# A decoder pipeline on one core: turned probabilities and FFN rows issued earlier in a step, and two clips done by GpSimd

## The reference, cut to what matters

```
x = x + tanh(g_xattn[2]) * L2_xattn(ln(x), ctx)   # 8 heads of 64, softmax over 64 context rows
x = x + tanh(g_ffn[2])   * L2_ffn(ln(x))          # bitlinear: w ternary, x rounded to 8 bits
x = x + tanh(g_xattn[3]) * L3_xattn(ln(x), ctx)
x = x + tanh(g_ffn[3])   * L3_ffn(ln(x))          # relu squared between two matmuls, plus a low-rank term

def act_quant(x):
    scale = 127.0 / clip(max(abs(x), axis=-1), EPS)
    return clip(round(x * scale), -128.0, 127.0) / scale
# L2_ffn: g = bitlinear(x, w_gate); u = bitlinear(x, w_up); bitlinear(relu(g)**2 * u, w_down)
```

## Time and profile before

| | |
|---|---|
| median of 3 runs | 1762.98 us (1762.85 to 1765.69) |
| the profiled execution's own time | 1767.82 us |
| its span | 1766.0 us |
| busy: PE, DVE, ACT, POOL | 1563.9 (89%), 1268.0 (72%), 847.1 (48%), 572.3 us (32%) |
| chain that ended last: PE, DVE, issue, ACT, POOL | 60%, 19%, 11%, 6%, 3% |
| 1300 to 1400 us, middle stage: PE, DVE, ACT, POOL busy | 82.55, 79.66, 57.07, 24.62 us |
| 1600 to 1700 us, late stage: PE, DVE, ACT, POOL busy | 89.89, 49.72, 45.77, 26.37 us |
| granted TensorE clock in both | 1.00 (1.00 is 2.4 GHz) |

### The profile page before, as it was taken

How to read it: one execution, slowest core, us unless ns; L and a number is a source line. 1 busy time by engine, 2 the same in 40 slices (tenths; PEclk the granted TensorE clock), 3 DMA queues, 4 the chain that set the end, 5 groups by cost and what they waited for, 6 DMA issues and landing times.

```text
span 1766.0 us, 36226 instructions
## 1 busy us (share of the span) xinstructions
PE 1563.9 (89%) x10771; PEld 1024.4 (58%) x10771; DVE 1268.0 (72%) x4952; ACT 847.1 (48%) x1721; POOL 572.3 (32%) x1090
## 2 busy tenths in 40 slices
PE   5999999998999698888889699988888888888898
PEld 4666666665666454554487456665555555555655
DVE  3888888887777699999936744436778788745454
ACT  4444444443555455555323255544555555544443
POOL 3434344343000356656235311113222222222221
PEclk8999999999999778878659899999999999999999
DMA  6000000000800000000010100000000000000000
GB/s 164 2 0 0 0 0 0 0 0 1 174 3 0 13 1 0 0 0 0 1 43 0 30 2 0 0 1 1 1 1 0 0 1 1 1 7 6 6 10 21
DMA packets 35288, 21.74 MB, mean 12 GB/s; under 512 B 19056, under 2 KB 32464, under 8 KB 35088
## 3 DMA queue, kind: packets, MB, share of 16 engines
q1 hardware_dynamic: 35216, 20.83, 5.0%
HBM read 16.63 MB, written 4.19 MB: 12 GB/s over the span
## 4 chain that ended last, share of the span: by engine, by line
PE 60%; DVE 19%; issue 11%; ACT 6%; POOL 3%; DVEq 1%; SPq 1%; DMA 0%; POOLq 0%; ACTq 0%
PE ps L695 7%; PE ps L704 7%; PE ps L372 6%; PE ps L388 6%; PE ps L2093 4%; DVE arena L1359 4%; PE ps L2088 4%; DVE arena L1353 4%; PE ps L402 3%; PE ps L415 3%; PE ps L2142 3%; PE ps L2153 2%; PE ps L2132 2%; PE ps L1696 2%; PE ps L435 1%
## 5 line engine op out<-in xcount | busy, mean ns | idle before, releaser
L2257 ACT COPY arena<-ps 128x512 f32<-128x512 f32 x128 | 75.1, 586 | 212.2 <-PE ps L2093 212.2
L2088 PE MATMUL ps<-arena 128*128 128x128 f32 x1024 | 137.0, 279 | 1.1 <-ACT arena L2291 0.5
L2093 PE MATMUL ps<-arena 128*64 128x512 f32 x512 | 135.7, 605 | 0.2 <-ACT arena L2257 0.2
L695 PE MATMUL ps<-xnT,arena 128*128 128x512 f32 x256 | 135.0, 620 | 0.0
L2088 PEld LDWEIGHTS ps<-arena 128*128 128x128 f32 x1024 | 125.9, 195 | 7.4 <-issue 4.8
L372 PE MATMUL ps<-arena 128*128 128x128 f32 x1024 | 122.8, 279 | 2.1 <-ACT arena L339 2.1
L388 PE MATMUL ps<-arena 128*64 128x512 f32 x512 | 122.3, 598 | 2.1 <-DVE arena L504 2.1
L372 PEld LDWEIGHTS ps<-arena 128*128 128x128 f32 x1024 | 121.7, 195 | 2.3 <-ACT arena L339 2.3
L2142 PE MATMUL ps<-arena 128*64 128x128 f32 x1024 | 70.0, 278 | 52.9 <-ACT arena L2303 52.9
L2533 POOL TENSOR_TENSOR ln_veps<-ln_mv,eps 128x1 f32<-128x1 f32 x64 | 12.3, 191 | 313.3 <-DVE ln_mv L2327 313.2
L1810 DVE TENSOR_SCALAR_CACHE_REDUCE thr_hits<-thr_abs,thr_candidate 128x512 bf16<-128x512 f32 (+1 forms) x248 | 102.0, 477 | 3.6
(11 more groups left out here) (413 smaller groups left out, 3915.4 us busy)
## 6 DMA issues: line engine op xcount, KB each, us to landing
toeplitz<-ssm_toeplitz_scratch SPq DMA_DIRECT2D x2, 2048.0 KB, 18.0
ssm_toeplitz_scratch<-ssm_padded_kernel SPq DMA_DIRECT2D x1, 2048.0 KB, 11.3
out<-x_res SPq DMA_DIRECT2D x8, 256.0 KB, 2.3
arena<-L_ffn_W SPq DMA_DIRECT2D x2, 512.0 KB
arena<-L_xattn_Wq SPq DMA_DIRECT2D x1, 512.0 KB
arena<-L_xattn_Wo SPq DMA_DIRECT2D x1, 512.0 KB
thr_abs<-L_ffn_W SPq DMA_DIRECT2D x2, 256.0 KB, 7.7
arena<-L_xattn_W SPq DMA_DIRECT2D x2, 256.0 KB
```

Of the source, the lines that this page charges most:

```text
L695: nc.tensor.matmul(ps[:, u % 3, :], w1[:, x, c * P:(c + 1) * P], xnT, start=True, stop=True).then_inc(h_full.sem, 1)
L2088: last = T_.matmul(ps[:, 1 - n, j * P:(j + 1) * P], folded[phase].mT[:, 4 * n + j, :], cg[:, s, :], start=True, stop=True)
L2093: last = T_.matmul(ps[64 * m:64 * m + 64, 4, :], cg[:, s, b * CTX:(b + 1) * CTX], folded[phase].wvo[:, m, :, :], start=True, stop=True)
L2257: S.copy(VW[:, r % 2, b, :, :].rearrange("p c d -> p (c d)"), ps[:, 4, :]).then_inc(v_laid.sem, 1)
```

## The change

P is issued after FFN2's gate and up matmuls and ahead of xn's transpose, and its copy right after the exponential. hT is issued ahead of the gate matmul, and its copy ahead of relu; FFN3's x copy moves ahead of the exponential. xn's transpose goes to the second part of bank 5, behind y; so y waits also for xn's copy of the step before, and xn's transpose for the x addition. The clips of h and of q leave VectorE for GpSimd: `clip_h` behind the two rstd instructions, `clip_q` at the end of a step's GpSimd work. The rounding instructions get waits for the clip before them. VectorE's aggregate moves from behind the subtraction to behind `round_h`.

```diff
@@ -2081,7 +2081,7 @@
         e.wait_ge(xn_done.sem, xn_done.at(t + 1))
-        T_.transpose(ps[:, 2, 0:P], xn[:, s, :], k.ident[:]).then_inc(xt_full.sem, 1)
+        T_.transpose(ps[:, 5, D:D + P], xn[:, s, :], k.ident[:]).then_inc(xt_full.sem, 1)
 
@@ -2137,6 +2137,7 @@
             e.wait_ge(x_done.sem, x_done.at(t - 2))
+            e.wait_ge(xt_laid.sem, xt_laid.at(t + 1 if r < STEPS else STEPS))
             for c in range(C):
@@ -2155,6 +2156,11 @@
             values(e, s, 1, phase)
+        if downs(r):
+            e.wait_ge(hq_done.sem, hq_done.at(t - F2))
+            for c in range(IC):
+                last = T_.transpose(bank16(0)[:, c * P:(c + 1) * P], hb[:, c * P:(c + 1) * P], identb[:])
+            last.then_inc(ht_full.sem, 1)
         if gates(r):
@@ -2167,27 +2173,29 @@
             hidden3(e, t, r, b)
-        pe_weights(e, r)
         if turns_x(r):
             e.wait_ge(n_out.sem, n_out.at(b - 1))
+            if downs(r):
+                e.wait_ge(ht_laid.sem, ht_laid.at(t - F2))
             for j in range(GT):
...
             last.then_inc(x3_full.sem, 1)
-            if downs(r):
-                e.wait_ge(x3_laid.sem, x3_laid.at(1))
+        pe_weights(e, r)
+        if 1 <= r < STEPS + 1:
+            e.wait_ge(s_prob.sem, s_prob.at(t))
+            e.wait_ge(p_laid.sem, p_laid.at(t - 1))
+            for c in range(C):
+                last = T_.transpose(ps[:, 2, c * P:(c + 1) * P], PR[:, o, 2 * c:2 * c + 2, :], k.ident[:])
+            last.then_inc(p_full.sem, 1)
         if turns_q(r):
             e.wait_ge(q_done.sem, q_done.at(b - 1))
-            e.wait_ge(g_laid.sem, g_laid.at(2 * t + 2))
+            if downs(r):
+                e.wait_ge(ht_laid.sem, ht_laid.at(t - F2))
             for j in range(GT):
...
             last.then_inc(qt_full.sem, 1)
-        if downs(r):
-            e.wait_ge(hq_done.sem, hq_done.at(t - F2))
-            for c in range(IC):
-                last = T_.transpose(bank16(0)[:, c * P:(c + 1) * P], hb[:, c * P:(c + 1) * P], identb[:])
-            last.then_inc(ht_full.sem, 1)
         if ahead(r, 1):
-            e.wait_ge(p_laid.sem, p_laid.at(t - 1))
+            e.wait_ge(x_done.sem, x_done.at(t - 1))
             turn_xn(e, t + 1, o)
@@ -2221,15 +2229,6 @@
             keys(e, t + 1, o, 1, (r + 1) // TILES)
-        if 1 <= r < STEPS + 1:
-            e.wait_ge(s_prob.sem, s_prob.at(t))
-            if ahead(r, 1):
-                e.wait_ge(xt_laid.sem, xt_laid.at(t + 2))
-            else:
-                e.wait_ge(p_laid.sem, p_laid.at(t - 1))
-            for c in range(C):
-                last = T_.transpose(ps[:, 2, c * P:(c + 1) * P], PR[:, o, 2 * c:2 * c + 2, :], k.ident[:])
-            last.then_inc(p_full.sem, 1)
 
@@ -2244,7 +2243,7 @@
         e.wait_ge(xt_full.sem, xt_full.at(t + 1))
-        S.copy(xnT[:, s * P:(s + 1) * P], ps[:, 2, 0:P]).then_inc(xt_laid.sem, 1)
+        S.copy(xnT[:, s * P:(s + 1) * P], ps[:, 5, D:D + P]).then_inc(xt_laid.sem, 1)
 
@@ -2267,6 +2266,9 @@
             copy_values(e, t, r, 1)
+        if downs(r):
+            e.wait_ge(ht_full.sem, ht_full.at(t - F2))
+            S.copy(hT[:], bank16(0)[:, 0:HID]).then_inc(ht_laid.sem, 1)
         if gates(r):
@@ -2276,16 +2278,16 @@
             relu3(e, t, r)
+        if turns_x(r):
+            e.wait_ge(x3_full.sem, x3_full.at(b - 9))
+            S.copy(x3T, ps[:, 0, :]).then_inc(x3_laid.sem, 1)
         if attend(r):
...
         act_weights(e, r)
-        if turns_x(r):
-            e.wait_ge(x3_full.sem, x3_full.at(b - 9))
-            S.copy(x3T, ps[:, 0, :]).then_inc(x3_laid.sem, 1)
-        if downs(r):
-            e.wait_ge(ht_full.sem, ht_full.at(t - F2))
-            S.copy(hT[:], bank16(0)[:, 0:HID]).then_inc(ht_laid.sem, 1)
+        if 1 <= r < STEPS + 1:
+            e.wait_ge(p_full.sem, p_full.at(t))
+            S.copy(PT[:, o, :, :].rearrange("p c q -> p (c q)"), ps[:, 2, :]).then_inc(p_laid.sem, 1)
         if turns_q(r):
@@ -2298,9 +2300,6 @@
             copy_keys(e, t + 1, o, 1)
-        if 1 <= r < STEPS + 1:
-            e.wait_ge(p_full.sem, p_full.at(t))
-            S.copy(PT[:, o, :, :].rearrange("p c q -> p (c q)"), ps[:, 2, :]).then_inc(p_laid.sem, 1)
         if r == F3:
@@ -2372,12 +2371,10 @@
         e.wait_ge(q_step.sem, q_step.at(n + 3))
+        e.wait_ge(q_done.sem, q_done.at(g))
         for j in range(GT):
...
         last.then_inc(q_step.sem, 1)
-        e.wait_ge(q_step.sem, q_step.at(n + 4))
-        e.wait_ge(qt_full.sem, qt_full.at(g))
-        V.tensor_scalar(qb[:], qf[:], -ROUND, 127.0, ALU.add, ALU.min).then_inc(q_done.sem, 1)
 
@@ -2388,11 +2385,23 @@
         e.wait_ge(a_recip.sem, a_recip.at(n))
+        if not (isinstance(n, int) and n < 2):
+            e.wait_ge(hq_done.sem, hq_done.at(n - 1))
         V.tensor_scalar(hq[:], h[:], sh[:, 0:1], ROUND, ALU.mult, ALU.add).then_inc(hr_done.sem, 1)
+
+    def clip_h(e, t):
+        n = t - F2
         e.wait_ge(hr_done.sem, hr_done.at(n))
...
             e.wait_ge(ht_full.sem, ht_full.at(n - 1))
-        V.tensor_scalar(hb[:], hq[:], -ROUND, 127.0, ALU.add, ALU.min).then_inc(hq_done.sem, 1)
+        e.nop(nofuse=True)
+        G_.tensor_scalar(hb[:], hq[:], -ROUND, 127.0, ALU.add, ALU.min).then_inc(hq_done.sem, 1)
+
+    def clip_q(e, g):
+        e.wait_ge(q_step.sem, q_step.at(4 * g + 4))
+        e.wait_ge(qt_full.sem, qt_full.at(g))
+        e.nop(nofuse=True)
+        G_.tensor_scalar(qb[:], qf[:], -ROUND, 127.0, ALU.add, ALU.min).then_inc(q_done.sem, 1)
 
@@ -2454,6 +2463,8 @@
             round_h(e, t)
+        if ahead(r, 2):
+            norm_aggregate(e, t + 2, r + 2)
         if 2 <= r < STEPS + 2:
@@ -2467,8 +2478,6 @@
                             mx[:, s, :].unsqueeze(2).to_broadcast([P, heads, CTX]), ALU.subtract).then_inc(s_sub.sem, 1)
-        if ahead(r, 2):
-            norm_aggregate(e, t + 2, r + 2)
         if norms(r, 0):
@@ -2538,6 +2547,8 @@
             norm_rstd(e, t + 2, r + 2)
+        if downs(r):
+            clip_h(e, t)
         if norms(r, 0):
@@ -2551,6 +2562,8 @@
                              ALU.mult).then_inc(s_prob.sem, 1)
+        if norms(r, 2) and r < LN3:
+            clip_q(e, b - 2)
```

## The result

The changed kernel takes 1800.79 us (median of 4 runs, 1798.29 to 1806.24), the one before 1763.5 beside it: ratio 1.0213, 95% interval 1.0187 to 1.0240. It is slower by some 37 us; the forecast was 33 us faster. The profiled execution took 1806.24 us with a span of 1804.4 (before: 1767.82 and 1766.0), so the two traces differ by 38.4 us, close to the medians.

What follows compares the result with a forecast made beforehand. It took TensorE's decoder steps, with waits before y and the down matmul, as the bound; gains of 7.7 early, 4.5 middle, 20.1 late and 1.0 tail sum to 33.3 us, so 1763.0 becomes 1729.7 us, range 1712 to 1748.

Steps and rivals of the forecast that it cites:

- the price of C: GpSimd's clip of h in the middle stage: C is its time, taken as 0.75 us, ends 0.47 and 1.27.
- rival 4: Middle-stage ring with a slow clip: slower kernel from C = 1.83 on, 1772 us at C = 2.1; chance 0.05.
- Rival 2: GpSimd's clip costs like a two-input instruction, 1.06 to 1.27 us: 10 to 16 us worse, 1739 to 1746; chance 0.2.
- the rstd link: Middle-stage stretch from VectorE's aggregate to the end of GpSimd's two rstd instructions, ahead of the clip: 1.01 us.
- The ring: Middle stage, hT(r) to hT(r+1) through ScalarE, VectorE and GpSimd: four steps take 32.4 us + 4C.
- rival 1: The ring doesn't bind in the middle stage, four steps take some 30 us: 39 us more gain, 1691; chance 0.08.
- P's saving: P in mid-step removes TensorE's wait before y: late 20.1 us, early 7.7, tail 1.0.
- Rival 3: Late stage doesn't give its microsecond, y's waits or the copies coming late: half of 20 us, 1740; chance 0.08.
- The SBUF port: GpSimd's clip holding up VectorE: taken as 0; hits on the roundings could cost up to 0.75 us each.
- hT sooner: Middle stage, hT ahead of the gate matmul with its clip on GpSimd: 0.6 us gained over 28 steps.
- The range: Whole kernel: 1712 to 1748 us, from C's ends (-9 to +16), ring sums (6) and early stage (3).

Runs made afterwards that it cites:

- e4: Changed kernel with 12 to 30 small matmuls whose results nobody reads ahead of TensorE's wait for hT: 1784.29 us.
- e12: Changed kernel with GpSimd's two-operation clip of h replaced by a plain GpSimd copy from f32 to bf16: 1738.44 us, ratio 0.9846.
- e5: Kernel before with only P and its copy sooner and xn's transpose in bank 5; hT, clips and aggregate as before: 1721.22 us.
- e8: Changed kernel with only h's clip given back to VectorE, q's clip staying on GpSimd: 1706.34 us, ratio 0.9657.
- e6: Kernel before with both clips on GpSimd, h's ahead of the rstd instructions, every order else as before: 1760.96 us.
- e3: Changed kernel with GpSimd's clip of h ahead of its two rstd instructions: 1756.38 us.
- e7: Changed kernel with h's clip cut in two, VectorE clipping columns 0 to 255, GpSimd 256 to 511: 1776.53 us.

## Why the prediction was wrong

The step that failed is "the price of C". It took C = 0.75 us with ends of 0.47 and 1.27; measured is 1.925, outside these ends. The neighbours were real rows but of other operations: a copy scaled to 512 elements gives about what a copy of 512 takes (0.61), and says nothing of a tensor_scalar. The forecast's upper end was the dearest GpSimd instruction of 512 elements in the trace, as if a kind that isn't in it couldn't cost more. Its own break-even, C = 1.83, was just below the truth, so rival 4, given 0.05, has the mechanism that happened, though not its size (it put 2.1 us at 1772). Rival 2, the same mechanism at up to 1.27, stopped short of it. The figure of the Trainium skill (GPSIMD Engine Reference, Performance versus the Vector engine), 769 ns for 512 elements, is near the copy (0.61 us) and far from this instruction (1.92).

The size follows, for 28 steps from y(11) to y(39), which took 307.6 us instead of 247.8, 59.8 more: C 28 x 1.175 = 32.9; the rstd link 28 x 0.16 = 4.5; the remaining 22.4 is 3.2 for each group of four, and the clock accounts for it: it costs 3.4 by the changed kernel's own steps at full clock, and e4 got at least 2.8 back. From y(39) to y(43) it was 46.4 instead of 34.8; C and the link are 5.3 of these 11.6, the rest wasn't taken apart.

- **The clock** was no term at all. The forecast let TensorE idle 1 us, up to 3, ahead of hT and priced the idle time as such only. Rival 4's line "each 0.1 us of C costs 3.1 us" gives 36 us for 1.175, so 1766; the kernel came out at 1801. Of the other 35, some 22 are the clock in those 28 steps (e4, which pays for its added matmuls, got 16 back), 5 the rstd link, 2 the smaller gains of the other stages, and the 6 that are left are about what steps 39 to 42 have unexplained.
- **The ring** was right, in its members and its sums: with C and the link as measured, within 0.12 us for each kind of step at full clock, and within 0.16 in each of four in e12. That it doesn't bind (rival 1) has fallen for this order; that it needn't be there, e5 shows.
- **P's saving** was right where TensorE is next: late 19.2 for 20.1, early 6.8 for 7.7, tail 0.4 for 1.0. Rival 3 has fallen.
- **The SBUF port** at 0 was nearly right. Most roundings took 0.49 us as in the earlier trace rows; the one in four that runs beside the last 0.3 us of q's clip took 0.52 to 0.57 (0.57 at 1323.63), so a hit cost under 0.1 us and not up to C. VectorE's normalisation at 1347.44 ran its 0.34 us inside the clip of 1346.84 to 1348.76, so it wasn't held up for the whole of it.
- **hT sooner** was judged to be worth 0.6 us in 28 steps. With the clip on VectorE, hT's move and what goes with it (the x copy, the aggregate, q's clip) are a real gain: e8 against e5, 15.6 us in the middle stage.
- **The range** had an error of its own: its terms (16, 6 and 3 us) add up to 1755 at the upper end, not 1748, while the lower end takes its terms in full. The measured time lies outside either.
- A clip that "exceeds 1 us" had been named as what would make the forecast wrong.

## What to carry to other kernels

An operation that no row shows has no upper bound from other operations, least of all when the path through it closes a ring. Then give the break-even price and a real chance to the far side of it, or don't centre on the cheap end. Before an instruction goes to another engine, ask what slack its consumer leaves: the same 1.92 us cost nothing in the order of before (e6) and for q (e8), and cost 94 us (1801 to 1706) in the one place where TensorE stands behind it in each step. And a wait of TensorE by 2 to 4 us a step may have to be priced twice, as idle time and as slower matmuls behind it: here the second price was 3.4 us in four steps, on top of 5.3 for the slower clip and link.

## What the runs showed of the hardware

- GpSimd at 512 f32 elements: copy 0.61 us, multiply of two inputs 1.26, tensor_scalar with one operation 1.50, with two 1.92; the output's type makes no difference.
- Pauses of TensorE of 1.97 to 3.88 us were followed by granted clocks of 0.55 to 0.61 for some 4 us in the changed kernel, yet pauses of 3.21 and 3.65 there, and of 2.51 and 3.03 in e3, were not. Filling the pauses with matmuls that nobody needs made the kernel 16 us faster.
- VectorE beside GpSimd: the normalisation of 128 elements took 0.34 us where the clip had 1.3 us or more still to run, as it does alone. In e7 it took 0.53 to 0.55 where 0.5 us of the clip was left (at 1337.97, beside the clip of 1337.34 to 1338.41). Why the place inside the clip matters isn't shown.
